# Padding of the expert lists from zeros of its own, idle tiles padded in the second batch, and new written orders

## The reference, cut to what matters

```python
h = _layernorm(x) * (1 + ca) + sa
x = x + ga * attention(h)              # 16 heads of 16, causal softmax, w_qkv, w_o
h = _layernorm(x) * (1 + cb) + sb
shared = (silu(h @ shared_w1.T) * (h @ shared_w2.T)) @ shared_w3.T
scores = sigmoid(h @ router_w.T)
top2   = top_k(scores + expert_bias, 2)            # of 8 experts
routed = sum over the two: w3[e] @ (silu(h1) * h2 * scores[e])   # h1, h2 = w12[e] @ h
x = x + gb * (shared + routed)
```

## Time and profile before

| | before |
|---|---|
| median of 3 runs | 1859.01 us |
| profiled execution | 1853.3 us |
| its span in the trace | 1851.6 us |
| TensorE busy | 1709.0 us (92%) |
| VectorE busy | 1532.0 us (83%) |
| ScalarE busy | 1077.3 us (58%) |
| GpSimd busy | 960.7 us (52%) |
| mean granted TensorE clock | 0.967 |

### The profile page before, as it was taken

How to read it: one execution, slowest core, us unless ns; L and a number is a source line. 1 busy time by engine, 2 the same in 40 slices (tenths; PEclk the granted TensorE clock), 3 DMA queues, 4 the chain that set the end, 5 groups by cost and what they waited for, 6 DMA issues and landing times.

```text
span 1851.6 us, 46100 instructions
## 1 busy us (share of the span) xinstructions
PE 1709.0 (92%) x17630; PEld 994.1 (54%) x17630; DVE 1532.0 (83%) x2761; ACT 1077.3 (58%) x1346; POOL 960.7 (52%) x1131
## 2 busy tenths in 40 slices
PE   5678889999999999999999999999999999899986
PEld 2233435545555455545454545454545878678664
DVE  7898999888988998898889888988885777556777
ACT  2568767666767676667667766767576332223221
POOL 2234356466545655555655556546466467445433
PEclk8689999999999999999999999999999999899998
DMA  4245321313131312122112212122123767767997
GB/s 148 54 134 154 86 58 49 70 38 105 29 82 28 96 43 65 31 88 53 54 48 71 53 54 65 53 60 65 53 66 104 179 137 159 167 139 158 286 302 275
DMA packets 214133, 183.14 MB, mean 99 GB/s; under 512 B 146640, under 2 KB 182232, under 8 KB 212128
## 3 DMA queue, kind: packets, MB, share of 16 engines
q1 hardware_dynamic: 200768, 143.87, 30.9%
q0 software_dynamic: 12960, 36.06, 6.0%
q10 hardware_dynamic: 192, 0.26, 0.1%
HBM read 65.23 MB, written 62.19 MB: 69 GB/s over the span
## 4 chain that ended last, share of the span: by engine, by line
PE 54%; DVE 14%; POOL 7%; DMA 5%; issue 5%; SPq 5%; ACT 4%; ACTq 0%; DVEq 0%; POOLq 0%
PE pair L1889 11%; PE pair L1897 11%; PE pair L1941 6%; PE pair L1867 6%; PE pair L1843 5%; DVE max_part L1329 5%; PE pair L1921 4%; POOL lists L992 3%; PE pair L1817 3%; PE pair L1932 2%; PE pair L1829 2%; PE pair L1967 2%; ACT arena L1139 2%; SPq L721 1%; ACT feat L1089 1%
## 5 line engine op out<-in xcount | busy, mean ns | idle before, releaser
L1139 ACT ACTIVATE arena<-pair 128x1024 f32<-128x1024 f32 (+1 forms) x640 | 572.5, 939 | 209.2 <-PE pair L1867 184.8
L1329 DVE TENSOR_REDUCE max_part<-pair 128x2 f32<-128x1024 f32 (+2 forms) x448 | 532.4, 1211 | 65.0 <-PE pair L1843 61.9
L1897 PE MATMUL pair<-feat_parts,ffn_sb 128*128 128x512 f16 x1536 | 377.3, 381 | 7.4 <-DVE arena L1551 4.2
L1889 PE MATMUL pair<-arena,v_sb 128*32 128x256 f32 (+1 forms) x5120 | 322.6, 373 | 3.3 <-DVE max_part L1329 1.2
L1843 PE MATMUL pair<-arena 48*128 48x128 f16 (+3 forms) x2304 | 204.2, 283 | 37.3 <-DVE max_part L1329 10.8
L1867 PE MATMUL pair<-arena 50*128 50x256 f16 (+1 forms) x2560 | 208.6, 265 | 29.9 <-DVE max_part L1329 12.7
L922 POOL TENSOR_SCALAR_AFFINE_SELECT arena<-arena 128x1024 f32<-128x1024 f32 x128 | 140.5, 1098 | 181.9 <-ACT arena L1121 181.9
L916 POOL TENSOR_SCALAR_AFFINE_SELECT arena<-arena 128x512 f32<-128x512 f32 x256 | 162.4, 648 | 136.5 <-ACT arena L1139 135.5
L1007 POOL DMA_INDIRECT slots<-arena,feat x142 | 142.9, 1006 | 157.4 <-DVE arena L1563 126.6
L1897 PEld LDWEIGHTS pair<-feat_parts,ffn_sb 128*128 128x128 f16 x1536 | 131.3, 98 | 173.6 <-issue 27.5
L1921 PE MATMUL pair<-parts,arena 128*128 128x256 f16 x1704 | 200.9, 277 | 12.2 <-DMA parts<-lists 8.8
(11 more groups left out here) (218 smaller groups left out, 2158.3 us busy)
## 6 DMA issues: line engine op xcount, KB each, us to landing
arena<-parts SPq DMA_DIRECT2D x380, 64.0 KB, 2.3
rows<-x SPq DMA_DIRECT2D x8, 1024.0 KB, 5.6
x_sb<-x SPq DMA_DIRECT2D x16, 512.0 KB, 4.7
base<-norm SPq DMA_DIRECT2D x14, 512.0 KB, 2.9
ffn_parts<-hidden SPq DMA_DIRECT2D x8, 768.0 KB, 4.1
arena<-ffn_parts SPq DMA_DIRECT2D x8, 768.0 KB, 6.4
x_sb<-ffn_w SPq DMA_DIRECT2D x6, 768.0 KB, 5.6
norm<-ffn_w SPq DMA_DIRECT2D x6, 768.0 KB, 7.4
```

Source lines behind the costliest of these rows:

```text
L1139: sc.activation(to[:, :, lo:QC], of[:, :, lo:QC], ACT.Exp, scale=SCALE / QK_SCALE ** 2).then_inc(exp_done, 1)
L1329: return vec.tensor_reduce(to, of, AX.X, ALU.max)
L1889: last = mm(to[32 * j:32 * j + 32, lo:QC], v_sb[:, kt, h:h + 32], probs[:, u % RING, at + lo:at + QC], start=(kt == 0), stop=(kt == 2 * c ...
L1897: last = mm(to[:, 0:512], w_up[s][W_PART[i]][:, f, m * RH + h * P:m * RH + (h + 1) * P], feat_parts[:, A_PART[i], f, c * 512:(c + 1) * 512 ...
```

## The change

1. `pad_zero` (128 x 264 f32) is a new SBUF tensor. GpSimd fills it, and `pad_known` (now 128 x 30 x 2), at the start of the kernel; `make_pads` and the step `pads` are gone.
2. `close:q` writes the padding of two experts only and waits for `tails_ready` alone.
3. All seven idle blocks are written in the stage "second", by two DMAs at `load_gates`: the first of 14 x 128 rows of 1056 bytes from one row of zeros per partition, read again and again; the second of 14 x 128 rows of 8 bytes.
4. All five written orders and all bank choices but those of the "start" stage are new. No step is added or removed but `pads`.

```diff
         pad_ids = sb("pad_ids", [P, PADS * RT], I32)
-        pad_known = sb("pad_known", [P, PADS, RT, 2], F32)
+        pad_known = sb("pad_known", [P, PADS * RT, 2], F32)
+        pad_zero = sb("pad_zero", [P, ID_AT // 2], F32)
...
-        pad_rows = rows32[:, 0:RT, :]
...
-        PADS_OUT = 16 * 2 * PADS
+        PADS_OUT = 16 * 2 * (NE + 1)
...
-            def pad(row, k):
-                sp.dma_start(list_rows(row)[:, :, 0:ID_AT // 2], pad_rows[:, :, 0:ID_AT // 2]).then_inc(pads_out, 16)
-                sp.dma_start(list_rows(row)[:, :, ID_AT // 2:], pad_known[:, k, :, :]).then_inc(pads_out, 16)
+            def pad(to, first, n):
+                sp.dma_start(to[:, :, 0:ID_AT // 2], pad_zero[:, :].unsqueeze(1).to_broadcast([P, n, ID_AT // 2])).then_inc(pads_out, 16)
+                sp.dma_start(to[:, :, ID_AT // 2:], pad_known[:, first:first + n, :]).then_inc(pads_out, 16)
...
                     elif kind == "close":
                         q = at[0]
-                        sp.wait_ge(pads_made, 3)
                         sp.wait_ge(tails_ready, 1)
                         for e in range(2 * q, 2 * q + 2):
                             row = sp.value_load(tails[0:1, e:e + 1], min_val=e * LIST, max_val=(e + 1) * LIST - ROWS)
-                            pad(row, e)
-                        for k in range(2 * q, min(2 * q + 2, IDLE_TILES)):
-                            pad(IDLE + k * ROWS, NE + k)
+                            pad(list_rows(row), e * RT, RT)
...
                         load_gates(b)
+                        if v == "second":
+                            sp.wait_ge(pads_made, 3)
+                            pad(list_dram[IDLE:LIST_ROWS, :].rearrange("(t p) d -> p t d", p=P), NE * RT, IDLE_TILES * RT)
...
             gp.tensor_copy(ident_b[:, :], ident[:, :]).then_inc(pool_set, 1)
+            gp.memset(pad_zero[:, :], 0.0).then_inc(pads_made, 1)
+            gp.memset(pad_known[:, :, :], 0.0).then_inc(pads_made, 1)
+            pool.wait_ge(pads_made, 2)
+            gp.tensor_copy(pad_known[:, :, 0:1], pad_ids[:, :].unsqueeze(2)).then_inc(pads_made, 1)
...
-            def make_pads():
-
-                pool.wait_ge(listed_done, 2 * B * LISTED)
-                gp.memset(pad_rows, 0.0).then_inc(pads_made, 1)
-                gp.memset(pad_known[:, :, :, :], 0.0).then_inc(pads_made, 1)
-                pool.wait_ge(pads_made, 2)
-                gp.tensor_copy(pad_known[:, :, :, :].rearrange("p k t c -> p (k t) c")[:, :, 0:1], pad_ids[:, :].unsqueeze(2)).then_inc(pads_made, 1)
```

Of the orders, the pieces of "end" that the prediction speaks of (each list is one text; line breaks are the text's own):

```diff
-        scatter:15 xr:26 tup:25 ty:23 xr:27 tlo:25 tup:26 tlo:26 close:0 pads ty:24 xr:28 tup:27 table_rest:1:0 tlo:27 ty:25 xr:29 tup:28 ty:26 xr:30 tup:29
-        tlo:28 tlo:29 ty:27 xr:31 tup:30 ty:28 ty:29 tlo:30 xr:32 xr:33 tup:31 tup:32 ty:30 tlo:31 tlo:32 close:1 xr:34 tup:33 up:1:0 up:1:1 tlo:33 hid:0
-        close:2 up:1:2 up:1:3 up:1:4 ty:31 up:1:5 up:2:0 up:2:1 hid:1 up:2:2 table_rest:1:1 ty:32 xr:35 xr:36 tup:34 tup:35 up:2:3 up:2:4 tlo:34 tlo:35 up:2:5
-        ty:33 close:3 ty:34 ty:35 xr:37 tup:36 xr:38 tup:37 tlo:36 tlo:37 up:3:0 up:3:1 xr:39 tup:38 up:3:2 tlo:38 up:3:3 ty:36 xr:40 hid:2 ty:37 xr:41 tup:39
...
-        ty:48 xr:52 tup:51 ty:49 xr:53 ty:50 tup:52 tlo:51 gate_rows tlo:52 xr:54 tup:53 ty:51 xr:55 ty:52 xr:56 tup:54 tlo:53 tlo:54 tup:55 ty:53 xr:57 ty:54
...
+        tup:22 scatter:9 tlo:21 close:0 scatter:10 ty:20 xr:24 tup:23 tlo:22 ty:21 xr:25 tup:24 scatter:11 scatter:12 scatter:13 scatter:14 tlo:23 tlo:24
+        ty:22 xr:26 tup:25 ty:23 xr:27 tup:26 tlo:25 tlo:26 ty:24 xr:28 tup:27 ty:25 xr:29 tup:28 up:1:0 tlo:27 tlo:28 ty:26 xr:30 tup:29 ty:27 xr:31 tup:30
+        tlo:29 ty:28 xr:32 tup:31 up:1:1 up:1:2 tlo:30 tlo:31 close:1 close:2 up:1:3 table_rest:1:0 up:1:4 ty:29 xr:33 tup:32 hid:0 ty:30 close:3 xr:34 ty:31
+        up:1:5 up:2:0 tup:33 up:2:1 up:2:2 up:2:3 up:2:4 tlo:32 table_rest:1:1 gate_rows xr:35 tup:34 tlo:33 ty:32 xr:36 tup:35 up:2:5 up:3:0 up:3:1 hid:1
+        tlo:34 tlo:35 up:3:2 scatter:15 ty:33 xr:37 tup:36 ty:34 xr:38 tup:37 ty:35 up:3:3 up:3:4 tlo:36 xr:39 tup:38 ty:36 tlo:37 tlo:38 xr:40 tup:39 up:3:5
```

and the piece of "second" with the new padding (`load_gates` was the last step of that stage before):

```diff
+        scores:52 ln:1 scores:53 max:3:15 values:49 values:50 values:51 raw:10 max:3:16 max:3:17 diag_max:3:14 shifts:3 scores:54 down:3:0 down:3:1 max:0:0
+        max:0:1 down:3:2 scores:55 scores:56 load_gates values:52 values:53 values:54 max:0:2 normalise:9 normalise:10 max:0:3 scores:57 select_max:0:1 up:8:0
+        up:8:1 up:8:2 up:8:3 up:8:4 up:8:5 max_turn:3 values:55 values:56 max:0:4 max:0:5 diag_max:0:1 up:9:0 up:9:1 up:9:2 hid:8 up:9:3 up:9:4 router:1
+        up:9:5 up:10:0 scores:58 scores:59 route:1 hid:9 qk:1 up:10:1 select_max:0:5 up:10:2 up:10:3 up:10:4 up:10:5 up:11:0 scores:60 max:0:6 up:11:1 up:11:2
```

More of the change, by code:

```diff
@@ L134 @@
[L134 to L149, removed]
@@ L157 @@
[L157 to L168, removed]
@@ L181 @@
-        max:0:15 max:0:16 scatter:8 scatter:9 raw:14 scatter:10 normalise:14 values:71 scores:73 up:13:0 up:13:1 up:13:2 up:13:3 scatter:11 scatter:12
-        scatter:13 scores:74 scatter:14 max:0:17 diag_max:0:14 values:72 scores:75 up:13:4 up:13:5 scores:76 scores:77 shifts:0 v:1 max_turn:0 values:73
-        scores:78 scores:79 scatter:15 hid:13 values:74 values:75 load_gates
+        osp:0 values:-4 select_max:1:1 select_max:1:5 osp:1 max:1:0 values:-3 max:1:1 max:1:2 max:1:3 values:-2 values:-1 raw:-1 max:1:4 max:1:5 scores:0
@@ new lines @@
+        scores:16 values:15 scores:17 scores:18 scores:19 values:16 normalise:1 ln:0 select_max:2:1 select_max:2:5 max:2:0 raw:2 max:2:1 max:2:2 values:17
+        values:18 values:19 raw:3 max_turn:1 max:2:3 max:2:4 max:2:5 diag_max:2:1 up:0:0 up:0:1 up:0:2 up:0:3 normalise:2 router:0 scores:20 scores:21 max:2:6
+        up:0:4 up:0:5 scores:22 scores:23 normalise:3 route:0 up:1:0 up:1:1 up:1:2 scatter:0 up:1:3 place:0 qk:3 rank:0 hid:0 up:1:4 up:1:5 up:2:0 scores:24
+        raw:4 values:20 values:21 scatter:1 up:2:1 scores:25 hid:1 scatter:2 max:2:7 max:2:8 up:2:2 values:22 values:23 values:24 scores:26 scatter:3
@@ L217 @@
+        diag_max:0:14 scores:74 v:1 scores:75 scores:76 shifts:0 values:72 values:73 scatter:12 scatter:13 scatter:14 scatter:15 scores:77 up:12:2 up:12:3
+        up:12:4 up:12:5 normalise:13 normalise:14 up:13:0 max_turn:0 hid:12 up:13:1 up:13:2 up:13:3 scores:78 scores:79 up:13:4 up:13:5 hid:13 values:74
+        values:75
     """,
     "last": """
-        osp:0 osp:1 osp:2 max:1:0 max:1:1 qk:2 scores:0 values:-4 values:-3 values:-2 values:-1 max:1:2 raw:-1 scores:1 scores:2 max:1:3 max:1:4 diag_max:1:1
@@ L232 @@
-        place:0 raw:6 rank:0 up:4:0 up:4:1 max:2:17 diag_max:2:14 scores:33 up:4:2 up:4:3 up:4:4 hid:3 shifts:2 normalise:5 normalise:6 up:4:5 scores:34
-        scatter:2 op:1 scores:35 up:5:0 scores:36 hid:4 rest:1 var:1 values:32 values:33 values:34 max:3:0 max:3:1 up:5:1 up:5:2 scores:37 up:5:3 up:5:4
-        table:0 max_turn:2 values:35 values:36 scores:38 max:3:2 scatter:3 scatter:4 select_max:3:1 up:5:5 up:6:0 up:6:1 up:6:2 up:6:3 scatter:5 scores:39
-        up:6:4 up:6:5 hid:5 scores:40 max:3:3 values:37 values:38 max:3:4 max:3:5 scores:41 up:7:0 up:7:1 scores:42 scores:43 diag_max:3:1 max:3:6 raw:7
@@ L240 @@
-        values:51 values:52 values:53 scores:56 max:3:15 max:3:16 normalise:9 ln:1 values:54 values:55 values:56 down:2:0 max:3:17 diag_max:3:14 shifts:3
-        raw:10 scores:57 down:2:1 down:2:2 router:1 down:3:0 down:3:1 scores:58 up:8:0 route:1 up:8:1 up:8:2 up:8:3 up:8:4 up:8:5 up:9:0 load_gates down:3:2
-        scores:59 max_turn:3 hid:8 scatter:8 place:1 rank:1 up:9:1 up:9:2 up:9:3 up:9:4 up:9:5 up:10:0 up:10:1 up:10:2 hid:9 up:10:3 up:10:4 up:10:5 up:11:0
-        scores:60 scores:61 values:57 values:58 values:59 scores:62 scores:63 up:11:1 up:11:2 values:60 normalise:10 values:61 scores:64 scores:65 raw:11
@@ new lines @@
+        up:5:0 hid:3 hid:4 rest:1 var:1 values:32 values:33 values:34 values:35 max:3:0 max:3:1 up:5:1 up:5:2 scores:37 up:5:3 up:5:4 max_turn:2 table:0
+        scores:38 select_max:3:1 max:3:2 up:5:5 up:6:0 up:6:1 up:6:2 up:6:3 values:36 values:37 scatter:2 scatter:3 scores:39 scores:40 up:6:4 up:6:5 max:3:3
+        hid:5 scores:41 scatter:4 values:38 max:3:4 max:3:5 diag_max:3:1 max:3:6 up:7:0 scores:42 scatter:5 scores:43 raw:7 up:7:1 fetch:1 up:7:2 raw:8
+        values:39 values:40 values:41 scores:44 normalise:7 up:7:3 up:7:4 norm2:1:0 scores:45 scores:46 normalise:8 scores:47 values:42 max:3:7 values:43
@@ new lines @@
+        shifts:3 down:3:0 down:3:1 router:1 scores:58 scores:59 up:8:0 route:1 max_turn:3 up:8:1 up:8:2 up:8:3 up:8:4 up:8:5 up:9:0 up:9:1 up:9:2 up:9:3
+        load_x:0 down:3:2 hid:8 up:9:4 fetch:2 load_gates up:9:5 up:10:0 up:10:1 place:1 rank:1 up:10:2 hid:9 up:10:3 up:10:4 up:10:5 scores:60 scores:61
+        values:57 values:58 values:59 normalise:10 scores:62 scatter:8 scatter:9 hid:10 scores:63 scores:64 values:60 values:61 scores:65 raw:11 raw:12
```

(1 more changed line is left out.)

237 lines of the change are left out of this document (128 added, 109 removed).

## The result

The changed kernel takes 1833.24 us (median of 4 runs, 1828.40 to 1835.14), the kernel before 1857.75 (4 runs, 1854.63 to 1861.08): a ratio of 0.9864 [0.9836, 0.9892] (in brackets its 95% interval), about 25 us faster, where 14.6 were forecast. A second set of runs of both gave 0.9862 [0.9841, 0.9883]. The profiled execution took 1835.05 us.

The account below looks back on a forecast made before the run. TensorE, busy 1709.0 of 1851.6 us, was taken as the bound, leaving its idle time and slow-clock stretches. 16.1 - 3 + 1.5 = 14.6 us off the 1859.0 median gave 1844.4; range 1837 to 1853, 8 in 10 1831 to 1861.

Parts of the forecast that it names:

- The padding: 16.1 us: Tile stage: 10.4 us from no longer waiting for GpSimd, plus 5.7 us from gaps behind the shorter closes.
- Its split: Padding gain divided: 10.4 us for the 7.86 us gap and slow matmuls behind it, 5.7 us for shorter closes.
- SyncE's new lateness: Tile loads around the closes and `gate_rows` come late from SyncE's issue time: bounds 0 to 9.2 us, 3 us lost.
- SyncE is late elsewhere: Rival, chance 0.15: closes, `gate_rows` or tile 41 make one new 10.4 us gap, 1852; with two, 1862.
- `gate_rows` leaves its old place: Before `xr:54`: the 1.53 us gap at 1703.96, behind a late load of scores, goes; 1.5 us gained.
- The new orders: All stages' new orders and banks: same work in another order, taken as 0 within plus or minus 6 us.
- The bound of 4.2 us a batch for the loop: Five loop batches: no more than 4.2 us each can be won, since TensorE is busy for the rest.
- the new orders win too: Rival, chance 0.16: the first attention batch gives back a third of its 32 us, 10.7, reaching 1834.
- The order of the tail: Last 131.6 us: full of DMA, but transfers start behind tile 55 and move up with the tiles; nothing counted.
- Setup, `scatter:15`, the burst: Zeros made at the start, the moved scatter and second-batch idle blocks: each taken as nothing; burst at worst 9 us.
- What would show it: Signs: no `pad_known` wait, no TensorE gap above 3 us between tiles 24 and 42, clock 1.00, loop batches at 176.3 us.

Follow-up runs that it names:

- changed, quarter of base: The changed kernel loading only a quarter of each base half in the output stage (14 loads of 128 KB, not 512): 1823.81 us, 0.9845.

## Why the prediction was right and where it was wrong

To place the gains I compared the times at which SyncE issues the same tile load: us ahead (-) of or behind (+) the first trace of the kernel before, at the loads that stood there at 1560, 1585, 1606 and 1630 us, at the one of 1764 (the last but two), and at the last store. The middle columns can be compared with the kernel before only where the order of the tiles is the one before, and are left out elsewhere. Worked out from the SyncE timelines:

```
                                   1560   1585   1606   1630   1764    end
before again                       +0.7   -0.1   -0.9   -1.0   -2.5   -4.0
new attention, old padding         -6.5   -7.1   -6.6   -7.0   -6.7   -8.2
own zeros, idle blocks at close    +1.5   -5.0   -7.0   -7.4   -4.3   -6.0
padding alone                      -0.8   -9.0  -13.2  -17.0  -13.8  -15.3
padding and new attention          -5.0  -13.1  -17.2  -21.2  -21.2  -21.6
old tiles, new tail                -5.9  -14.1  -18.3  -22.2  -21.8  -26.6
old tiles, new tail, again         -8.6  -16.8  -20.9  -24.4  -24.4  -31.4
changed                                                       -11.4  -18.3
changed, again                                                -16.6  -23.4
changed, quarter of base                                      -17.6  -25.1
changed, old attention                                        -10.2  -13.7
changed, gate_rows late                                       -21.3  -22.2
changed, gate_rows late, again                                -23.3  -29.9
```

*The padding: 16.1 us before the new lateness. Right, and where the profile had it.* In the four kernels with the new padding and the old tile order the lead grows in three steps: by 8.1 or 8.2 us at `close:0`, 4.1 or 4.2 at the next close, 3.5 to 4.0 at the last, 15.8 to 16.3 us in all. In kernels with the old padding it does not grow by more than 1.7. By time it is 15.6 us.

*Its split was wrong.* I took 10.4 us for the wait and, net of the new lateness, 5.7 - 3 = 2.7 for the shorter closes. Measured by time: 5.6 and 10. The steps of the lead between the loads of 1560 and 1630 divide it more evenly, 8.9 for the wait (from +1.5 to -7.4) and 16.2 - 8.9 = 7.3 for the idle blocks; 2.3 us of the difference between the two traces stood there before the first close. Either way the wait got too much and the closes too little. The trace with the idle blocks still in the closes says why. Once GpSimd's zeros are out of the way, `close:0` is still 5.4 us long there (1567.38 to 1572.77) and leaves a gap of its own, 1.28 us, and the 3.32 us behind `close:3` stays. The 7.86 us gap had two causes one behind the other, and I gave all of it to the one that ended last. That the whole comes out at 16 all the same is no luck: it is the sum of the gaps and slow matmuls that stood there, and all of them went. Of the lead of the kernel with the idle blocks in the closes, 3.1 us is lost again between the loads of 1630 and 1764; the padding alone loses 3.2 there too. The kernels that have new attention as well lose nothing there; why is open.

*SyncE's new lateness: 3 us.* With the old tile order it is nothing, as the gaps are gone altogether. With the new one there is the gap in front of the tile whose load stands behind `gate_rows`: 1.2 to 3.4 us, and in two of four traces slow matmuls with it. That is the "SyncE is late elsewhere" rival at a small price, and with another mechanism: `gate_rows` waited for no padding (its first DMA followed the load before it by 0.12 us), but the load behind its 1 MB arrived late. The issue time in a row that the rival put at 26 us is 19.1, from 1587.91 to 1606.99. (A gap of 10.4 us in place of 3 is 7.4 us less, not the 7.2 written there; the 1852 stands.)

At the load of 1764 the kernels with new attention and the new tile order lead by 11.4, 16.6 and 17.6 us (mean 15.2), those with the old tile order by 21.2, 21.8 and 24.4 (mean 22.5), and those with `gate_rows` late by 21.3 and 23.3. Not all of these 7 us belong to the tiles: at the last shift row of attention (1400 us in the trace before) the leads were 8.0, 7.2 and 9.0 against 9.8, 9.4 and 12.2. The place of `gate_rows` is best read from the load in front of it, the one of 1606, up to which the changed kernel and `gate_rows` late have one order: from there to 1764 the lead grows by 8.6, 11.4 and 10.4 us with it early and by 13.6 and 13.9 with it late, so 3 to 4 us. By time, 1829.25 us is 0.9867 where the changed kernel has 0.9864, and 1824.23 stands 3.6 us under its 1827.84. The size isn't settled.

*`gate_rows` leaves its old place: 1.5 us.* The gap went, but not for that reason. In the two traces with `gate_rows` back before `xr:54` TensorE waits there for at most 0.25 us, as in the changed kernel, and in all eight traces with the old order of the tiles up to there the gap stands at 1.2 to 2.4 us. It hangs on the order of the steps around it; which of them is open. The forecast's 1.5 us came true by luck.

*The new orders: "I take 0, within plus or minus 6 us". This is the step that failed.* New attention orders alone gave 7.8 us, and 0.9871 / 0.9916 = 0.9955 gives 8.3 on top of the padding. The term was put at nothing for want of a row that bounds a loss. The bound of 4.2 us a batch for the loop held. What was won there is small and repeats: TensorE's waits for the maxima in the loop, changed kernel,

```profile
PE pair L1862 <- DVE max_part L1324: 5.5, 11, 0.7
PE pair L1800 <- DVE max_part L1324: 2.8, 5, 0.6
```

where the trace before has 8.7 us at 20 places and 3.2 at 5; other waits there grew, and a batch came out near 0.4 us shorter, 2 us for five. The rest lies in `first`, `second` and `last`, at 1 to 2 us each by the mean progress of the shift rows, each no larger than what one trace differs from the next. No run changed one of these stages alone, so the split among them, and the waits that went in the three, are not shown. My own bound was too narrow: the four stages idle 32, 10.8, 21 and 5.5 us, and a tenth of that is 7 (reckoned afterwards; no run shows that a tenth is the rule). The rival "the new orders win too" had the right sign, but put it all into `first`, which gave about 1 us and not 10.7.

*The order of the tail.* I said nothing would be given back or won behind tile 55. Behind the load of 1764, six of eight traces with the new tail gain 4.8 to 7.6 us more (two only 0.9 and 3.5), those with the old tail 0.4 to 1.7. By time this gain doesn't show: the old tiles with the new tail are at 0.9872, the old tiles with the old tail at 0.9871. TensorE's waits in the last 122 us of the changed kernel:

```profile
PE pair L1927 <- DVE arena L1546: 5.6, 2, 3.9
PE pair L1936 <- POOL hidden L1010: 4.9, 1, 4.9
PE pair L1892 <- DVE silu_h L1379: 1.0, 1, 1.0
PE pair L1916 <- ACT silu_h L1154: 0.7, 1, 0.7
```

They and two more of 0.2 us come to 12.6 us; the like list of the trace before comes to 16.6, among it 4.2 us before the `up` matmuls that is now gone. So by the traces `end` loses in the tiles and wins in the tail, and by time it comes out near zero; that the two cancel is read from single traces and not shown by time.

*Setup, `scatter:15`, the burst: nothing, and so it was.* SyncE issues its first shift row 0.2 us earlier than before. No gap of TensorE stands at tile 41. The burst shows on SyncE's own timeline:

```profile
336.50 0.58 SPq L661 DMA_DIRECT2D gates_sb<-gates  x1
337.14 0.42 SPq L704 DMA_DIRECT2D lists<-pad_zero  x1
337.60 2.88 SPq L705 DMA_DIRECT2D lists<-pad_known  x1
342.23 4.52 SPq L678 DMA_DIRECT2D arena<-shift_rows  x2
```

Its second DMA held the queue for 2.88 us and the two shift rows behind it took 4.52 us to issue (1.34 at this place in the trace before), yet between the shift rows that stood at 346 and at 384 us before, the changed kernel and the one with new attention and no burst move alike: their leads change by 3.8 and 3.9 us. The nearer end of 0 to 9 us was the right one.

*What would show it.* Wait for `pad_known` gone: yes. No gap above 3 us between tiles 24 and 42, clock 1.00: only with the old tile order or `gate_rows` late; the changed kernel had 3.37 us and 0.98. Loop batches at 176.3 us: 0.4 us less.

By medians the account closes: 15.6 (padding) + 8 (attention orders) + 1 or 2 (order of `end`, not told from nothing) = 25 us, against 16.1 - 3 + 1.5 + 0 forecast. The best medians, beside the changed kernel's on the same chip, are those of `gate_rows` late and of the old tile order with the new tail, 3.6 and 5.5 us lower, but their intervals overlap it, so a better version is possible and not shown.

## What to carry to other kernels

A gap that ends with one late wait may hold a second cause behind it: before giving the whole gap to the wait, work out when the released instructions would have landed without it, here 5.4 us of padding issues on the same queue. Pieces that nobody needs soon, issued one by one in the queue that feeds the tiles, cost 10 us by time (7.3 by the steps of the lead) where the same packets in a stretch with slack cost nothing that the traces show. A large transfer issued just ahead of a load that is soon needed can make that load late even if the queue itself waits for nothing: here the load behind 1 MB took 5.8 to 7.7 us to arrive. And where every written order is new, the stages' idle time is worth a share and not zero: here four stages gave 8 us together.

## What the runs showed of the hardware that was not expected

Issuing one DMA of 14 x 128 packets of 8 bytes right behind one with as many of 1056 bytes held SyncE for 2.88 us (2.88 to 2.99 in all ten traces that have it) against about 0.4 for the small ones, and in the eight of them where two shift rows came next, these took 3.95 to 4.52 us to issue and not 1.34. Taking 5.5 MB out of a stretch whose DMA engines read 1.03 busy lowered that to 0.89 and the time by 4 us by medians, with intervals that overlap: a full DMA row in the profile did not mean here that the transfers alone set the end. And two traces of one kernel lie up to 7.7 us apart in span (1828.2 and 1833.3 us for the changed kernel, 1821.7 and 1829.4 with `gate_rows` late, these two on different chips), while the steps at the three closes agreed within 0.5 us in four traces: differences of a few us are read as steps of the lead, not from the spans.
